# Reordering the turn from projections to attention in a transformer-layer kernel on one core

## What is computed

```python
x = layernorm(hidden)
q = rms_norm(x @ Wq + bq, gq)          # over all 4096 columns of the 32 heads
k = rms_norm(x @ Wk + bk, gk)
v = x @ Wv + bv
...
attn = softmax(q @ k.T / sqrt(128))    # per batch and head, 512 x 512
out = (attn @ v).reshape(B, S, 4096) @ Wo + bo
x = hidden + layernorm(out)
```

## Time and profile before

| | |
|---|---|
| time, median of 3 runs | 1101.89 us (1100.92 to 1103.08) |
| the profiled execution's own time | 1103.57 us |
| its span | 1101.5 us |
| TensorE matmul busy | 1062.8 us, 96% |
| VectorE busy | 794.2 us, 72% |
| ScalarE busy | 727.3 us, 66% |
| GpSimd busy | 678.6 us, 62% |
| phase A / turn / phase B, about | 0 to 340 / 340 to 425 / 425 to 1045 us |
| feed-forward | 1045 us to the end |

### The profile page before, as it was taken

How to read it: one execution, slowest core, us unless ns; L and a number is a source line. 1 busy time by engine, 2 the same in 40 slices (tenths; PEclk the granted TensorE clock), 3 DMA queues, 4 the chain that set the end, 5 groups by cost and what they waited for, 6 DMA issues and landing times.

```text
span 1101.5 us, 19973 instructions
## 1 busy us (share of the span) xinstructions
PE 1062.8 (96%) x5724; PEld 577.2 (52%) x5724; DVE 794.2 (72%) x1801; ACT 727.3 (66%) x1427; POOL 678.6 (62%) x593
## 2 busy tenths in 40 slices
PE   6999999999999799999999999999999999999896
PEld 3444444444444465555555555555555555555385
DVE  7867666666644777777777777777777777777886
ACT  3567666666655677776777777777777677767432
POOL 2578767667665376766766666666667667664413
PEclk9999999999999899999999999999999999999998
DMA  6777755655664388687766766775775775776502
GB/s 232 167 264 244 241 219 198 228 217 199 234 147 131 108 210 211 185 175 171 190 171 168 194 172 162 193 177 157 191 183 155 191 182 159 184 167 150 162 1 76
DMA packets 311635, 197.39 MB, mean 179 GB/s; under 512 B 275248, under 2 KB 279216, under 8 KB 311472
## 3 DMA queue, kind: packets, MB, share of 16 engines
q1 hardware_dynamic: 311600, 196.97, 64.5%
HBM read 94.14 MB, written 35.68 MB: 118 GB/s over the span
## 4 chain that ended last, share of the span: by engine, by line
PE 63%; issue 14%; POOL 14%; DVE 4%; DMA 2%; ACT 2%; POOLq 1%; SPq 0%; DVEq 0%
PE ps L1095 21%; PE ps L1096 21%; PE ps L1097 21%; POOL acc L582 10%; POOL qk_out L573 3%; DMA vo_top_scratch<-top_o 1%; DVE stats L1429 1%; DMA wv_stage<-w_vo 1%; DVE y L1908 1%; POOL wb_lo L727 0%; DMA y<-x 0%; DVE y L1794 0%; DVE ps L1811 0%; ACT pair_q L926 0%; ACT ps L917 0%
## 5 line engine op out<-in xcount | busy, mean ns | idle before, releaser
L1811 DVE TENSOR_SCALAR_CACHE_REDUCE ps<-ps,score_down 128x512 f32<-128x512 f32 x256 | 177.6, 756 | 95.3 <-PE ps L1097 94.8
L1825 DVE SCALAR_TENSOR_TENSOR pair_q<-ps,row_inv,pair_q 128x512 f16<-128x512 f32 x256 | 174.6, 744 | 56.7 <-ACT pair_q L926 54.4
L1095 PE MATMUL ps<-xh,wa_hi 128*128 128x512 f16 x512 | 195.0, 381 | 6.1 <-DVE qk_out L1639 3.8
L917 ACT ACTIVATE ps<-ps,neg_max 128x512 f32<-128x512 f32 x256 | 168.2, 657 | 48.1 <-DVE ps L1811 48.1
L1097 PE MATMUL ps<-xh,wa_lo 128*128 128x512 f16 x512 | 195.1, 381 | 0.0
L1096 PE MATMUL ps<-xl,wa_hi 128*128 128x512 f16 x512 | 195.1, 381 | 0.0
L926 ACT ACTIVATE pair_q<-ps,row_inv 128x512 f16<-128x512 f32 x256 | 154.9, 688 | 20.2 <-DVE row_inv L1818 19.9
L675 POOL CAST oth<-o_t 128x512 f16<-128x512 f32 x62 | 37.8, 610 | 210.1 <-ACT o_t L902 210.1
L582 POOL TENSOR_TENSOR acc<-acc,squares 128x512 f32<-128x512 f32 x120 | 150.1, 1272 | 0.0
L1095 PE MATMUL ps<-wv_hi,xh 128*128 128x256 f16 x512 | 139.6, 273 | 0.0
L1097 PE MATMUL ps<-wv_hi,xl 128*128 128x256 f16 x512 | 139.6, 273 | 0.0
(11 more groups left out here) (184 smaller groups left out, 2221.8 us busy)
## 6 DMA issues: line engine op xcount, KB each, us to landing
q_k_scratch<-qk_out SPq DMA_DIRECT2D x64, 512.0 KB, 4.0
qk_in<-q_k_scratch SPq DMA_DIRECT2D x64, 512.0 KB, 3.4
wa_stage<-w_qk SPq DMA_DIRECT2D x32, 512.0 KB, 4.0
u_stage<-w_vo SPq DMA_DIRECT2D x32, 512.0 KB, 5.0
wv_stage<-w_vo SPq DMA_DIRECT2D x16, 512.0 KB, 4.2
wo_stage<-w_vo SPq DMA_DIRECT2D x16, 512.0 KB, 4.1
qk_tops<-qk_top_scratch SPq DMA_DIRECT2D x28, 128.0 KB, 4.6
y<-x SPq DMA_DIRECT2D x8, 256.0 KB, 5.5
```

The lines of the kernel that those rows point to most:

```text
L917: act.activation(ps[:, SCORE + i, :], ps[:, SCORE + i, :], ACT.Exp, bias=neg_max[:, sl, i:i + 1], scale=-1.0, accum_out=row_sum[:, sl, i:i ...
L1095: pe.matmul(outp, lhs[0], rhs[0], start=first, stop=False)
L1811: dve.tensor_scalar(ps[:, SCORE + i, :], ps[:, SCORE + i, :], score_down[:, sl, i:i + 1], None, ALU.mult, ALU.min, accum_out=neg_max[:, sl ...
L1825: dve.scalar_tensor_tensor(out=pair_q[:, 1, i, :], in0=ps[:, SCORE + i, :], scalar=row_inv[:, sl, i:i + 1], in1=pair_q[:, 0, i, :], op0=AL ...
```

## The change

No instruction is added or taken away; the order in the turn and one wait of TensorE differ.

```diff
             # SyncE
-            for s in range(2):
-                load_qk(0, s)
+            load_qk(0, 0)
             sp.wait_ge(o_top_ready, 1)
             sp.dma_start(vo_top_scratch[1], top_o[:, :]).then_inc(o_top_stored, 16)
-            for s in range(2, 4):
-                load_qk(0, s)
+            load_qk(0, 1)
             sp.wait_ge(o_top_stored, 16)
             sp.dma_start(tops_o[:, :], vo_top_scratch[1:2].broadcast_to([P, P])).then_inc(o_tops_loaded, 16)
             sp.wait_ge(wv_lo_ready, 2)
             sp.dma_start(wv_stage[:, :, :].rearrange("p c n -> p (c n)"), w_vo[1]).then_inc(wv_loaded, 16)
+            for s in range(2, 4):
+                load_qk(0, s)
...
             # ScalarE
-                if pos == 4:
-                    act.wait_ge(wv_loaded, 32)
-                    split_wv(1, 1, 0)
-                    split_wv(1, 1, 2)
...
                 evacuate_v(1, 0, VB)
+                act.wait_ge(wv_loaded, 32)
+                split_wv(1, 1, 0)
+                split_wv(1, 1, 2)
...
                 split_wo(0, 0, 0)
+                evacuate_v(3, 4, VB)
                 output(0, 2)
                 high_k(2, 2)
-                spread(1, VB)
+                spread(1, YB + 1)
                 split_wo(0, 0, 1)
-                evacuate_v(3, 4, YB + 1)
+                evacuate_v(4, 6, YB)
...
-                evacuate_v(4, 6, YB)
...
             # TensorE
                 if pos == 0 or pos == 2:
                     pe.wait_ge(wa_lo_ready, 2 * (HEADS - 1 + par))
-                    pe.wait_ge(k_out_ready, 2 * (HEADS - 3 + par))
+                if pos % 2 == 0:
+                    pe.wait_ge(k_out_ready, 2 * (HEADS - 3 + par) - 1 + g // 2)
...
             pe.wait_ge(k_out_ready, 2 * HEADS)
             pe.wait_ge(vl_ready, 2)
+            v_item(0, 4, VB)
             attend(0, 0, 0)
-            spread(1, VB)
-            pe.wait_ge(var_ready, 6)
-            v_item(0, 4, YB + 1)
+            spread(1, YB + 1)
+            v_item(0, 6, YB)
             pe.wait_ge(qk_lo_ready, 3)
             scores(2, 2)
-            v_item(0, 6, YB)
+            pe.wait_ge(wv_lo_ready, 4)
+            pe.wait_ge(vl_ready, 3)
+            v_item(1, 0, VB)
             pe.wait_ge(otl_ready, 1)
             attend(1, 1, 0)
             pe.wait_ge(rms_row_ready, 2)
-            pe.wait_ge(wv_lo_ready, 4)
-            v_item(1, 0, VB)
             pe.wait_ge(qk_lo_ready, 4)
             scores(3, 3)
...
             # VectorE
-            dve.wait_ge(stored[0][1], 16 * (PAIRS - 1))
-            store_k(0, 1, 2, 8 * PAIRS - 2)
...
             first_keys(0, 4)
+            first_low_k(0)
+            dve.wait_ge(stored[0][1], 16 * (PAIRS - 1))
+            store_k(0, 1, 2, 8 * PAIRS - 2)
             out_factors()
-            first_low_k(0)
-            low_wv(1, 0)
...
             split_v(1, 0, VB)
-            low_wv(1, 2)
+            low_wv(1, 0)
...
-            low_wo(0)
-            first_keys(1, VB)
+            low_wv(1, 2)
+            split_v(3, 4, VB)
+            first_keys(1, YB + 1)
             dve.wait_ge(rms_ready, 2)
             scores_down(2, 0, 0, 1)
             first_low_k(1)
-            low_wo(1)
-            split_v(3, 4, YB + 1)
+            low_wo(0)
+            split_v(4, 6, YB)
             maxima(2, 0)
             inverses(2, 0)
             for i in range(TB):
                 low_halves(2, 0, i)
             scores_down(3, 1, 1, 1)
-            split_v(4, 6, YB)
+            low_wo(1)
             step(0, 3, 0, rows=False)
```

## The result

The changed kernel took 1106.78 us (median of 12 runs, 1102.95 to 1108.27), the kernel before 1101.62 us beside it (12 runs, 1098.58 to 1105.58). The ratio is 1.0044 with a 95% interval of 1.003 to 1.0059: 3.3 to 6.5 us slower. The forecast was 1103.5 us and no difference, with a range up to 1106.2: the median lies above the range, on the side of the slower rival.

A forecast was written before the change was run, and what follows sets the result against it. TensorE bounds the kernel, without room from 425 to 1010 us, so only the turn counts: -6.5, -1.9, +1.2, +0.8, +6.1, +1.9 give +1.6 us on 1101.89, forecast 1103.5 us, range 1098.5 to 1106.2.

The forecast's parts named there:

- no difference: Whole kernel: the gain at the keys is given back at `attend(2)`, result within 2.2 us (0.2%); chance 0.47.
- the slower rival: Start of `attend(2)`: step 2's transposes queue behind all three transfers, X = 406.7, +3.3 us, 1105.2 us; chance 0.33.
- Part 1: Keys awaited by batch, before the column sums: no gain, but a clock fall after them costing 1.2 us, bounds 0 and 1.9.
- Part 4: Values ahead of attending: 1.08 us wait and slow matmuls stay; `rows` waits 0.8 us for `low_wo(1)`, taken at 1.5 us.
- Part 2: Second pair's values split moved: ScalarE's 8.2 us wait goes, step 0 scores start 6.5 us earlier, clock saves 1.9 more.
- What is late next: SyncE's queue behind `load_wo(0)`: step 2's transposes land late, TensorE idles 6.1 us before `attend(2)`, slow clock adds 1.9.
- X: The start of `attend(2)`, taken as 405.1; the result is X - 405.3 + 1.9, deciding for slower from 405.6 on.
- Part 3: SyncE's keys behind the stores: the store of `top_o` may be faster than 9.41 us; worth 0, bounds 0 and 0.5.
- The sum: All terms at the end of `attend(2)`, against the profiled execution: +1.6 us, reaching the kernel's end.
- the whole gain stays: Step 2's transposes not late at all, so 7.2 us or more remain: 1094.7 us; chance 0.06.

## Why the prediction was wrong

The mechanism forecast was in the main the one that happened: a gain at the keys, given back at `attend(2)` by transposes that are late behind `load_wo(0)`. Three sizes were too small: the time of the transposes behind three transfers (taken 7.3 us, measured 10.0), the slow clock behind them (1.9, measured 2.3) and the price of Part 1 (1.2, measured 2.3 on average). Together they moved the result out of "no difference" and out of the range. The reason given for the wait of `rows` was wrong too (Part 4).

**Part 2** was right. `scores` of step 0 was put 24.5 us after the mark by the prediction (357.7 - 333.16); with the clock held and the old key wait it came at 24.4, in three profiles. With the clock fallen it came at 26.1 to 28.2; with the 1.2 us of Part 1 the prediction had it at 25.7. The move alone made the kernel 8.2 us faster.

**What is late next** is the step that failed, in its size. The prediction took 7.3 us from the first issue to the landing of the second transpose, from the pair at 417.53 and 420.88, where one load stood ahead. Three stood ahead here. Measured were 10.0 us. The issue of the first transpose took 1.57 us where six us had passed since the last transfer, 3.23 with one just ahead, 5.5 to 6.0 with three, in all six profiles of kernels with the late low half and the old queue. The prediction had the three transfers in view and used a row with one, against which it set half of the bytes of the other two as its upper bound. That all three go first was the slower rival: from 397.9 to its X of 406.7 are 8.8 us, by the rule 9.1, both nearer to 10.0 than the 7.3. The Trainium skill ("DMA: Bandwidth & Descriptors", Queues, rings and completion order) has the descriptors of one issuing queue consumed in ring order on each DMA engine. These traces agree with it: the key load landed at 400.3 and the first transpose, issued 0.6 us behind it, only at 394.14 + 8.2 = 402.3. A nearer row was in the trace of the kernel before, at the first transpose of step 3. There the issue of the last of three transfers of 512 KB ends 3.75 us ahead of it:

```profile
402.66 0.51 SPq L402 DMA_DIRECT2D q_k_scratch<-qk_out  x1
403.22 0.43 SPq L457 DMA_DIRECT2D qk_in<-q_k_scratch  x1
403.70 0.83 SPq L490 DMA_DIRECT2D wv_stage<-w_vo  x1
408.28 1.90 SPq L498 DMA_TRANSPOSE pair_k<-pair_q  x1
```

The issue of the transpose ends 5.65 us after that of the third transfer (404.53 to 410.18). In all profiles with three such transfers ahead, in step 2 or step 3, the issue is the shorter the longer the gap to the third: 5.5 to 6.0 us after a gap of 0.2, 4.5 to 5.0 after 1.0 to 1.1, 2.4 to 2.8 after 2.6 to 2.9, 1.8 to 1.9 after 3.8 to 4.0. Gap and issue together are 5.3 to 6.2 us each time; only behind a gap of six us is 1.57 left. With the 5.65 us of this row the prediction's own sum gives, as an estimate, 397.9 + 5.7 + 0.1 + 4.0 = 407.7 for X, on the slower side.

The term came out as 7.77 us idle, where 6.1 was forecast, although `low_wo(1)` took only 0.74 us (taken: 1.5), which let SyncE go earlier than forecast. Behind it the slow matmuls cost 4.9 - 2.6 = 2.3 us (forecast 1.9).

**Part 1** failed in size too. The prediction took 1.2 us and bounded it at 1.9. It missed two things. GpSimd's sums take 5.37 to 5.39 us instead of 4.94, in all six profiles with the new wait; the column sums start 16.5 us after the mark instead of 16.05. That this is VectorE's `wv_lo` beside them is argued from the two rows that overlap (VectorE's own two also rose, from 2.34 to 2.5 and 2.6 us); no run takes the overlap away alone. And the idle time is 3.2 us in five of six profiles, where the prediction had counted 1.9, and there the clock falls already within the column sums. The 1.52 and 0.24 us of before and the 0.45 us make 2.2 of it; where the other 1.0 us comes from stays open. In the sixth, the profile above, TensorE came late and idled 1.07 us; there the clock held and `scores` came at 24.8. Over six profiles with the new wait `scores` of step 0 starts on average 27.3 us after the mark (24.8 to 28.2), over five with the old one 25.1 (24.4 or 26.1). The price is 2.3 us on average and 3.8 at most. The runs say the same: 1110.43 against 1106.6 us, and 1096.48 against 1093.93. In both pairs the intervals of the ratios overlap, so I don't rest the size on them alone.

**Part 3** held at 0. The issue behind the store of `top_o` follows it by 8.0 us (340.02 to 348.05) where it took 9.4 before, and no wait of TensorE hangs on it.

**Part 4** held: 1.25 us in front of the values for 1.08 before, and `rows` waits 1.20 us for 0.8. It is released by GpSimd's `otl`, not by `low_wo(1)`, which was done at 392.6, so the reason was wrong and the size came near by luck. `low_wo(1)` has a part in it all the same: `otl` started 0.14 us after it and took 1.61 us, where it took 1.16 with the low half early. Behind the second lull twelve matmuls took 4.08 us before, and 24 of 256 columns take 4.23 now: the clock costs there what it cost, to 0.1 us, as forecast.

ScalarE waits 5.9 us for the same late load of the output weights, to 397.6, ahead of step 3's exponentials. That was seen and priced at nothing, and TensorE, idle to 404.25 for the transposes, indeed has no wait from it.

**The sum** of the profile shown: -6.2 and -1.8 at the keys, 1.2 for `rows`, 7.8 for the transposes, 2.3 for the clock there, 0.1 for the clock at the second lull, 0.2 for the wait ahead of the values, and 0.3 for the edges of the two new waits (idle time is counted from the end of a 0.38 us row, though the next matmul could start 0.216 us after its start). That is 3.9 us, as the marks give. The forecast was +1.6. In the profile shown the clock behind the first column sums held; in the others `scores` of step 0 came 1.7 to 3.3 us later yet.

Of the rivals, "slower" was the right one. Its point of decision was X = 405.6, 72.4 us after the mark; in three profiles of the changed kernel `attend(2)` starts 73.7 to 76.6 after it. That the whole gain stays (0.06) was wrong. With `low_wo(1)` early the wait is 0.52 us, though that kernel is only 2.4 us faster than before; the move of the split alone is 8.2.

What stays open: why the clock falls behind the first column sums in three of eight profiles with the old key wait and holds in the others, with 0.24 us idle and the same sums ahead of it in each. And the issue time with transfers ahead is only described: no run here varies their size.

## What to carry to other kernels

When an edit moves the signal that releases a DMA queue, list all that stands behind the waiting entry in that queue, and price the latency of what matters by everything issued just ahead of it: here three 512 KB transfers turned a 1.6 us transpose issue into 6 us, and the gain from an early wait of 8 us that was removed did not show until they were out of the way. Look for a row in which as much stands ahead as will stand there: one with a single transfer ahead priced this one 2.7 us too low. Taking away a wait of TensorE that only lets it run ahead to the next one has a price too: the idle time collects in one piece, and here that cost the clock, so that the program with one wait more was the faster one.

## What the runs showed of the hardware

- The issue of a DMA transpose on SyncE is long when transfers stand ahead in its queue: 1.57 us with none issued in the six us before, 3.23 with one 512 KB transfer just ahead, 5.5 to 6.0 with three. With three it shrinks with the time since the last of them was issued, to 1.90 us after 3.75.
- Beside VectorE's low halves, GpSimd's work grew by the same 0.45 us in both places: the four sums 4.94 to 5.39, `otl` 1.16 to 1.61. VectorE's `wo_lo` was short (0.74) where it began first, and 1.64 where it began in the middle of GpSimd's work.
- After 3.17 to 3.19 us idle and the single-column matmuls the clock fell in five profiles of five, already within them; after 1.07 us idle it held in the one there is; after 0.24 us idle and the same matmuls it fell in three of eight, later and at a lower price: `scores` of step 0 came 1.7 us later by it, where it was 3.3 us in four of the five.
